# Attention layers 0 and 1: score stacks stored by half groups, loaded in rows of 8 KB

## The chip, the cores and the metric

The kernel runs on one core of one Trainium2 chip. The core has five engines with queues of their own: TensorE (PE, with its weight loads PEld), VectorE (DVE), ScalarE (ACT), GpSimd (POOL) and SyncE (SP), and 16 DMA engines. Transfers are issued by SP, ACT and POOL. The metric is the time of one execution on the device in microseconds (us), as the median of several.

## The reference

Four layers of gated cross-attention, each followed by a feed-forward part, over x of (32, 128, 128) in float32. What the change touches is the attention of layers 0 and 1 only: 16 heads of 8 elements, keys and values from the context, queries from the normalised x. Layer 0 turns queries and keys by their place (rotary), layer 1 does not.

```
q = proj(layernorm(x), Wq, bq)      # (32, 16, 128, 8)
k = proj(ctx, Wk, bk)
v = proj(ctx, Wv, bv)
attn = softmax(einsum('bhqd,bhkd->bhqk', q, k) / sqrt(8))
x = x + tanh(g) * (merge(attn @ v) @ Wo.T + bo)
```

## The kernel before

The 32 sequences are worked on in 8 groups (NG) of 4 (GS); a group has T = 512 columns, and HALF = 256 columns are two of its sequences. `heads_attention` is called once for layer 0 (`l0x`, with rope) and once for layer 1 (`l1x`). The five engines run programs written out by hand in this function, and meet by semaphores.

**Parts.** Scores are computed in bfloat16 at the precision of float32: keys and queries are each split into three bfloat16 parts (NPART = 3), and all nine products of a key part and a query part are summed in one matmul with a contraction over 3 x 3 x 8 = 72 rows (SROWS). So for each head a "stack" of 72 partitions is wanted, in which row (a, b, d) of the key stack holds part a of the keys and the same row of the query stack holds part b of the queries, for element d of the head. Three more rows (TROWS = 75) carry the negated maxima in the query stack, and ones in the key stack.

**How a stack is made.** The projection stands in `parts` as 128 partitions (d, head) x 3 parts x 512 columns. The reordering goes through DRAM. SP stores the parts into `scratch` and loads the stack from there. Keys are stored three times (L278), so that their three copies of a part lie where one load of 72 rows (L290) finds them; queries are stored once (L281), and a load of 24 rows is issued three times (L296). A load is made for each half group, and moves pieces of 256 columns of a head, 512 bytes. In SP's program for each group after the first stand: key store, key load of half 0, query store, query load of half 0, key load of half 1, query load of half 1. The load waits until the store of the whole group has landed (`s_stored`), and for the scores that read the same buffer two groups earlier (L288). In group 0 both key loads stand ahead of the query store, and after its loads of layer 0 SP issues the remaining 2.5 MB of x and context (L2740, L2745).

**Who uses it.** PE computes scores (L373: queries stationary, keys moving) three sequences ahead (LEAD), DVE takes the row maxima from them (L710), POOL splits the maxima into parts (L629 to L632), PE turns them (L399), ACT copies them out (L520) and issues a transfer of three rows into the query stack (L525). Then PE computes the transposed scores with the maxima already subtracted (L386), ACT takes the exponentials (L531), and PE multiplies by the values (L410). POOL splits the keys and queries of later groups (L615 to L621); in group 0 DVE does so (L698 to L703). `scores` waits at the first unit of each half group for `stack_landed` of keys and queries, and PE works strictly in order: everything behind a waiting L373 waits too.

Of the kernel before, what the change touches and what calls it, by code (L numbers as in the profile page):

```python
# [21 lines left out]
P = 128  # L22
# [143 lines left out]
def heads_attention(nc, k, name, rope, gain):  # L166
# [9 lines left out]
    with ExitStack() as ctx:  # L176
# [17 lines left out]
        parts = {n: sb(f"{n}_parts", [P, NPART, T], BF16) for n in "kq"}  # L194
        scratch = {"k": nc.dram_tensor(f"{name}_k_scratch", (2, NPART, NPART, P, T), BF16).ap(),
                   "q": nc.dram_tensor(f"{name}_q_scratch", (2, NPART, P, T), BF16).ap()}
        stack = {n: sb(f"{n}_stack", [TROWS, 2, HEADS, T], BF16) for n in "kq"}
        ones_row = sb("ones_row", [NPART, T], BF16)
# [31 lines left out]
        s_split = sem("split_step")  # L230
        s_stored = {n: sem(f"{n}_parts_in_dram") for n in "kq"}
        s_stack = {n: [[sem(f"{n}_stack_in_{p}_{hf}") for hf in range(2)] for p in range(2)] for n in "kq"}
# [20 lines left out]
        half = lambda hf: slice(hf * HALF, (hf + 1) * HALF)  # L253
        loads = {"k": 1, "q": NPART}
        stores = {"k": NPART, "q": 1}

# [3 lines left out]

        def parts_stored(eng, n, g):

            eng.wait_ge(s_stored[n], 16 * stores[n] * (g + 1))

# [3 lines left out]
        def _(sp):  # L268
            sp.wait_ge(s_fill, 4)
            sp.dma_start(stack["k"][SROWS:TROWS, :, :, :].rearrange("a p h t -> a (p h) t"),  # L270
                         bcast(ones_row[:, :].unsqueeze(1), [NPART, 2 * HEADS, T])).then_inc(s_ones, 16)

            def store(n, g):

                sp.wait_ge(s_parts[n], g + 1)
                if n == "k":
                    for b in range(NPART):
                        sp.dma_start(scratch["k"][g % 2, :, b].rearrange("a p t -> p a t"), parts["k"][:, :, :])\  # L278
                          .then_inc(s_stored["k"], 16)
                else:  # L280
                    sp.dma_start(scratch["q"][g % 2].rearrange("b p t -> p b t"), parts["q"][:, :, :])\  # L281
                      .then_inc(s_stored["q"], 16)

            def load(n, g, hf):

                parts_stored(sp, n, g)
                if g >= 2:
                    sp.wait_ge(s_T, 4 * (GS * (g - 2) + 2 * hf + 2))  # L288
                if n == "k":
                    sp.dma_start(stack["k"][0:SROWS, g % 2, :, half(hf)],  # L290
                                 scratch["k"][g % 2].rearrange("a b (d h) t -> (a b d) h t", h=HEADS)[:, :, half(hf)])\
                      .then_inc(s_stack["k"][g % 2][hf], 16)
                else:
                    rows_of_a = NPART * HD
                    for a in range(NPART):
# [23 lines left out]
        def _(pe):  # L319
# [43 lines left out]
            def scores(j, u):  # L363

                g, c = divmod(j, GS)
                if u == 0 and c % 2 == 0:
                    stack_landed(pe, "k", g, c // 2)
                    stack_landed(pe, "q", g, c // 2)
                if 4 * j + u >= 2:
                    pe.wait_ge(s_max, 4 * j + u - 1)  # L370
                for i in range(4):
                    h = 4 * u + i
                    ins = pe.matmul(bankS[u % 2][:, seq(i)], stack["q"][0:SROWS, g % 2, h, seq(c)],  # L373
                                    stack["k"][0:SROWS, g % 2, h, seq(c)], start=True, stop=True)
                ins.then_inc(s_S, 1)

            def scoresT(j, u):
# [6 lines left out]
                for i in range(4):  # L384
                    h = 4 * u + i
                    ins = pe.matmul(bankT[u % 2][:, seq(i)], stack["k"][:, g % 2, h, seq(c)],  # L386
                                    stack["q"][:, g % 2, h, seq(c)], start=True, stop=True)
                ins.then_inc(s_T, 1)
# [96 lines left out]
        def _(act):  # L485
# [36 lines left out]
            def max_rows(j):  # L522
                g, c = divmod(j, GS)
                act.wait_ge(s_mT, j + 1)
                act.dma_start(stack["q"][SROWS:TROWS, g % 2, :, seq(c)], mT[:, seq(c)]).then_inc(s_mrow[c], 16)  # L525

# [63 lines left out]
        def _(pool):  # L590
# [2368 lines left out]
```

## Time and profile before

| | |
|---|---|
| median of 3 runs | 1749.2 us (1742.07 to 1757.42) |
| the profiled execution | 1753.31 us, span 1751.5 us |
| granted TensorE clock over the span | 0.869 of full |
| busy: PE, DVE, ACT, POOL | 1434.0, 901.2, 510.1, 413.7 us |
| attention of layer 0 in the trace | from the start to about 265 us |
| attention of layer 1 | about 430 to 668 us |
| DMA | 134171 packets, 151.33 MB |

The remaining time belongs to the feed-forward parts and to layers 2 and 3. A wait of an engine is named by the line that waited and by what came last; "issue" there means that the profile found no releaser. The landing of the stack loads is not recorded for the loads of the later groups, only their issue on SP.

### The profile page before, as it was taken

How to read it: one execution, taken by the hardware profiler on the slowest of the kernel's cores; microseconds unless marked ns; L12 is line 12 of the kernel's file. 1: busy time of each engine (PE TensorE's matmuls, PEld its weight loads, DVE VectorE, ACT ScalarE, POOL GpSimd, SP SyncE). 2: the span in 40 equal slices, each digit the busy share in tenths (PEclk: the TensorE clock that was granted, in tenths of full speed). 3: DMA queues.
4: the chain of work that ended last, by engine and by line, in shares of the span. 5: the costliest groups of instructions: out<-in, count | busy, mean ns of one | idle time of the engine just before them, and what ended most of it. 6: DMA issues, size and time to landing. Idle time of an engine off the chain costs nothing. (4 is left out here: it accounts for less than half of the span.)

```text
span 1751.5 us, 26351 instructions
## 1 busy us (share of the span) xinstructions
PE 1434.0 (82%) x8869; PEld 909.0 (52%) x8869; DVE 901.2 (51%) x2554; ACT 510.1 (29%) x1195; POOL 413.7 (24%) x713
## 2 busy tenths in 40 slices
PE   4798886885688885897778669666699999999998
PEld 2577663443467673665677547444344443444443
DVE  4565646886356552433354433375544465455535
ACT  1455552111366652222443223243010110111001
POOL 2665710000466520000133322262000000000000
PEclk8698988997599877999575679888799999999999
DMA  6665650000667636700000011123222022022110
GB/s 179 170 160 136 147 132 1 1 0 7 170 154 165 155 87 241 312 0 8 23 19 20 21 46 56 46 66 109 97 97 103 1 102 103 25 78 103 60 43 12
DMA packets 134171, 151.33 MB, mean 86 GB/s; under 512 B 12150, under 2 KB 117942, under 8 KB 128806
## 3 DMA queue, kind: packets, MB, share of 16 engines
q1 hardware_dynamic: 127494, 142.28, 27.6%
q0 software_dynamic: 3296, 6.76, 1.3%
q8 instruction: 68, 1.11, 0.3%
q10 hardware_dynamic: 3264, 0.79, 0.2%
q14 instruction: 49, 0.40, 0.1%
HBM read 99.33 MB, written 49.48 MB: 85 GB/s over the span
## 5 line engine op out<-in xcount | busy, mean ns | idle before, releaser
L2596 DVE TENSOR_TENSOR l3f_weighted_T<-l3f_w_e,l3f_xnT 128x512 f32<-128x512 f32 x128 | 88.4, 691 | 129.8 <-PE psum L2347 115.0
L2347 PE MATMUL psum<-l3f_weighted_T,w_l3f_q 128*128 128x512 f32 x256 | 133.7, 604 | 16.2 <-DVE l3f_weighted_T L2596 14.4
L2347 PE MATMUL psum<-l3f_weighted_T,w_l3f_k 128*128 128x512 f32 x256 | 131.6, 596 | 0.0
L2347 PE MATMUL psum<-l3f_weighted_T,w_l3f_v 128*128 128x512 f32 x256 | 131.5, 595 | 0.0
L710 DVE TENSOR_REDUCE l1x_minus_max<-psum 128x4 f32<-128x512 f32 x128 | 85.9, 687 | 81.0 <-PE psum L373 79.7
L2356 PE MATMUL psum<-l3f_weighted_T,w_l3f_o 128*128 128x512 f32 x256 | 124.4, 624 | 1.7 <-DVE l3f_weighted_T L2596 1.7
L710 DVE TENSOR_REDUCE l0x_minus_max<-psum 128x4 f32<-128x512 f32 x128 | 85.4, 686 | 66.5 <-PE psum L373 65.9
L2596 DVE TENSOR_TENSOR l3f_weighted_T<-l3f_w_e,l3f_oT 128x512 f32<-128x512 f32 x128 | 88.4, 692 | 57.3 <-PE psum L2356 30.0
L531 ACT ACTIVATE l0x_probsT<-psum 128x512 f32<-128x512 f32 x128 | 73.6, 595 | 57.2 <-PE psum L386 49.8
L111 POOL TENSOR_TENSOR l3f_ln_rstd<-l3f_ln_mean_var,eps 128x4 f32<-128x4 f32 x8 | 1.9, 243 | 355.5 <-DVE l3f_ln_mean_var L104 355.5
L531 ACT ACTIVATE l1x_probsT<-psum 128x512 f32<-128x512 f32 x128 | 73.7, 593 | 36.4 <-PE psum L386 26.9
L2356 PEld LDWEIGHTS psum<-l3f_weighted_T,w_l3f_o 128*128 128x128 f32 x256 | 39.3, 188 | 82.9 <-DVE l3f_weighted_T L2596 78.2
L2347 PEld LDWEIGHTS psum<-l3f_weighted_T,w_l3f_k 128*128 128x128 f32 x256 | 48.9, 191 | 61.8 <-issue 61.8
L2347 PEld LDWEIGHTS psum<-l3f_weighted_T,w_l3f_v 128*128 128x128 f32 x256 | 48.9, 191 | 61.8 <-issue 61.8
L2347 PEld LDWEIGHTS psum<-l3f_weighted_T,w_l3f_q 128*128 128x128 f32 x256 | 44.6, 192 | 60.4 <-issue 44.4
L373 PE MATMUL psum<-l0x_k_stack,l0x_q_stack 72*128 72x128 bf16 x512 | 59.7, 250 | 15.9 <-DMA l0x_q_stack<-l0x_q_scratch 8.8
L373 PE MATMUL psum<-l1x_k_stack,l1x_q_stack 72*128 72x128 bf16 x512 | 57.7, 245 | 17.1 <-issue 10.4
L386 PE MATMUL psum<-l1x_q_stack,l1x_k_stack 75*128 75x128 bf16 x512 | 54.7, 237 | 2.3 <-DMA l1x_q_stack<-l1x_minus_max_T 2.3
L386 PE MATMUL psum<-l0x_q_stack,l0x_k_stack 75*128 75x128 bf16 x512 | 56.2, 241 | 0.5 <-DMA l0x_q_stack<-l0x_minus_max_T 0.5
L373 PEld LDWEIGHTS psum<-l0x_k_stack,l0x_q_stack 72*128 72x128 bf16 x512 | 41.5, 114 | 19.5 <-issue 16.2
L373 PEld LDWEIGHTS psum<-l1x_k_stack,l1x_q_stack 72*128 72x128 bf16 x512 | 40.1, 110 | 21.2 <-issue 18.4
L902 ACT ACTIVATE l0f_hT<-psum,w_l0f_cb 128x512 f32<-128x512 f32 x32 | 22.0, 687 | 99.3 <-PE psum L850 99.3
(480 smaller groups left out, 3034.5 us busy)
## 6 DMA issues: line engine op xcount, KB each, us to landing
l3f_w_e<-l3f_weights_scratch SPq DMA_DIRECT2D x32, 1024.0 KB, 4.6
sorted_x<-zeros SPq DMA_DIRECT2D x1, 16896.0 KB, 59.0
l0x_k_scratch<-l0x_k_parts SPq DMA_DIRECT2D x24, 384.0 KB, 3.8
l0x_k_stack<-l0x_k_scratch SPq DMA_DIRECT2D x16, 576.0 KB
l0x_q_stack<-l0x_q_scratch SPq DMA_DIRECT2D x48, 192.0 KB
l1x_k_scratch<-l1x_k_parts SPq DMA_DIRECT2D x24, 384.0 KB, 4.6
l1x_k_stack<-l1x_k_scratch SPq DMA_DIRECT2D x16, 576.0 KB
l1x_q_stack<-l1x_q_scratch SPq DMA_DIRECT2D x48, 192.0 KB
```

What stands on the lines that cost most here:

```text
L111: pool.tensor_tensor(k.rstd[:, :], k.mv[:, :, 1], k.eps[:, :], ALU.add).then_inc(k.s_vare, 1)
L373: ins = pe.matmul(bankS[u % 2][:, seq(i)], stack["q"][0:SROWS, g % 2, h, seq(c)], stack["k"][0:SROWS, g % 2, h, seq(c)], start=True, stop= ...
L386: ins = pe.matmul(bankT[u % 2][:, seq(i)], stack["k"][:, g % 2, h, seq(c)], stack["q"][:, g % 2, h, seq(c)], start=True, stop=True)
L531: act.activation(pT[:, j % 2, 4 * u:4 * u + 4, :], bankT[u % 2].rearrange("p (i q) -> p i q", i=4), ACT.Exp, scale=scale).then_inc(s_exp, 1)
L710: dve.tensor_reduce(nm[:, j % GS, 4 * u:4 * u + 4], bankS[u % 2].rearrange("p (i t) -> p i t", i=4), AX, ALU.max, negate=True).then_inc(s_ ...
L902: act.activation(hT[:, par, n, :], bankH[n % 2][:, :], ACT.Silu, bias=w["l0f_cb"][:, n:n + 1]).then_inc(r_act.sem, 1)
L2347: ins = pe.matmul(bank[:, :], w[name][:, e, :], xe[:, e % 2, :], start=(e == 0), stop=(e == NE3 - 1))
L2356: pe.matmul(bankO[g % 2][:, :], w["l3f_o"][:, e, :], xe[:, e % 2, :], start=(e == 0), stop=(e == NE3 - 1))\
L2596: dve.tensor_tensor(xe[:, e % 2, :], wE[:, g % 2, e, :], src, ALU.mult).then_inc(s_xe, 1)
```

## The change

Scratch and stacks get a dimension for the half group, so that all 16 heads of one half stand side by side: 16 x 256 columns of bfloat16 are one row of 8 KB, both in DRAM and in a partition of the stack. Stores go out by halves, each with a semaphore of its own. Keys are stored once. Queries are stored as five blocks, parts 0, 1, 2, 0, 1. A load of a half is three transfers of 24 rows for keys as for queries: for the keys three times parts 0, 1, 2; for the queries blocks s to s + 2, so parts (0, 1, 2), (1, 2, 0), (2, 0, 1). The nine pairs are complete, in another order. The matmuls read the same columns of a head from their new place.

```
-        scratch = {"k": nc.dram_tensor(f"{name}_k_scratch", (2, NPART, NPART, P, T), BF16).ap(),
-                   "q": nc.dram_tensor(f"{name}_q_scratch", (2, NPART, P, T), BF16).ap()}
-        stack = {n: sb(f"{n}_stack", [TROWS, 2, HEADS, T], BF16) for n in "kq"}
+        blocks = {"k": NPART, "q": 2 * NPART - 1}
+        scratch = {n: nc.dram_tensor(f"{name}_{n}_scratch", (2, 2, blocks[n], P, HALF), BF16).ap() for n in "kq"}
+        stack = {n: sb(f"{n}_stack", [TROWS, 2, 2, HEADS, HALF], BF16) for n in "kq"}
...
-                if n == "k":
-                    for b in range(NPART):
-                        sp.dma_start(scratch["k"][g % 2, :, b].rearrange("a p t -> p a t"), parts["k"][:, :, :])\
-                          .then_inc(s_stored["k"], 16)
-                else:
-                    sp.dma_start(scratch["q"][g % 2].rearrange("b p t -> p b t"), parts["q"][:, :, :])\
-                      .then_inc(s_stored["q"], 16)
+                for hf in range(2):
+                    to = scratch[n][g % 2, hf].rearrange("a p t -> p a t")
+                    sp.dma_start(to[:, 0:NPART, :], parts[n][:, :, half(hf)]).then_inc(s_stored[n][hf], 16)
+                    if n == "q":
+                        sp.dma_start(to[:, NPART:2 * NPART - 1, :], parts["q"][:, 0:NPART - 1, half(hf)])\
+                          .then_inc(s_stored["q"][hf], 16)
...
-                parts_stored(sp, n, g)
+                parts_stored(sp, n, g, hf)
...
-                if n == "k":
-                    sp.dma_start(stack["k"][0:SROWS, g % 2, :, half(hf)],
-                                 scratch["k"][g % 2].rearrange("a b (d h) t -> (a b d) h t", h=HEADS)[:, :, half(hf)])\
-                      .then_inc(s_stack["k"][g % 2][hf], 16)
-                else:
-                    rows_of_a = NPART * HD
-                    for a in range(NPART):
-                        sp.dma_start(stack["q"][a * rows_of_a:(a + 1) * rows_of_a, g % 2, :, half(hf)],
-                                     scratch["q"][g % 2].rearrange("b (d h) t -> (b d) h t", h=HEADS)[:, :, half(hf)])\
-                          .then_inc(s_stack["q"][g % 2][hf], 16)
+                rows_of = lambda ap: ap.rearrange("a (d h) t -> (a d) (h t)", h=HEADS)
+                block_rows = NPART * HD
+                for s in range(NPART):
+                    first = s if n == "q" else 0
+                    sp.dma_start(stack[n][s * block_rows:(s + 1) * block_rows, g % 2, hf, :, :]
+                                 .rearrange("r h t -> r (h t)"), rows_of(scratch[n][g % 2, hf, first:first + NPART]))                      .then_inc(s_stack[n][g % 2][hf], 16)
...
-                    ins = pe.matmul(bankS[u % 2][:, seq(i)], stack["q"][0:SROWS, g % 2, h, seq(c)],
-                                    stack["k"][0:SROWS, g % 2, h, seq(c)], start=True, stop=True)
+                    ins = pe.matmul(bankS[u % 2][:, seq(i)], stack["q"][0:SROWS, g % 2, c // 2, h, of_seq(c)],
+                                    stack["k"][0:SROWS, g % 2, c // 2, h, of_seq(c)], start=True, stop=True)
```

The transposed scores (L386) and ACT's transfer of the maxima (L525) are addressed in the same manner. POOL's wait for the stores of the group before (in `split`) becomes two waits, one for each half.

SP's queue at the start of layer 0, groups 0 and 1, before; `l0x_k_parts` are the split keys in SBUF, `l0x_k_scratch` their place in DRAM, and the numbers are partitions or rows x pieces x elements:

```order
L278 DMA l0x_k_scratch<-l0x_k_parts 128x3x512 x3
L290 DMA l0x_k_stack<-l0x_k_scratch 72x16x256 x2
L281 DMA l0x_q_scratch<-l0x_q_parts 128x3x512
L296 DMA l0x_q_stack<-l0x_q_scratch 24x16x256 x6
L2740 DMA x_sb<-in_x 128x2560
L2745 DMA ctxT<-in_ctxT 128x2560
L278 DMA l0x_k_scratch<-l0x_k_parts 128x3x512 x3
L290 DMA l0x_k_stack<-l0x_k_scratch 72x16x256
L281 DMA l0x_q_scratch<-l0x_q_parts 128x3x512
L296 DMA l0x_q_stack<-l0x_q_scratch 24x16x256 x3
```

The same place of the change:

```order
L279 DMA l0x_k_scratch<-l0x_k_parts 128x3x256 x2
L293 DMA l0x_k_stack<-l0x_k_scratch 24x4096 x6
L279 DMA l0x_q_scratch<-l0x_q_parts 128x3x256
L281 DMA l0x_q_scratch<-l0x_q_parts 128x2x256
L279 DMA l0x_q_scratch<-l0x_q_parts 128x3x256
L281 DMA l0x_q_scratch<-l0x_q_parts 128x2x256
L293 DMA l0x_q_stack<-l0x_q_scratch 24x4096 x6
L2737 DMA x_sb<-in_x 128x2560
L2742 DMA ctxT<-in_ctxT 128x2560
L279 DMA l0x_k_scratch<-l0x_k_parts 128x3x256 x2
L293 DMA l0x_k_stack<-l0x_k_scratch 24x4096 x3
```

The order of the kinds is unchanged. In each group SP issues 2 key stores instead of 3, 6 key loads instead of 2, 4 query stores instead of 1, and 6 query loads as before: 18 transfers instead of 12. The rows of PE, ACT, DVE and POOL stand in the same order before and after.

## Rows read from the trace of the kernel before

**Rows 1.** Waits, PE, 28 to 265 us: us in total, times, longest.
```profile
PE psum L373 <- DMA l0x_q_stack<-l0x_q_scratch: 8.8, 1, 8.8
...
PE psum L373 <- issue: 6.1, 2, 4.0
```

**Rows 2.** Waits, PE, 425 to 668 us.
```profile
PE psum L373 <- issue: 10.4, 3, 4.1
...
PE psum L373 <- DMA l1x_q_stack<-l1x_q_scratch: 5.6, 1, 5.6
...
PE psum L386 <- DMA l1x_q_stack<-l1x_minus_max_T: 2.3, 2, 1.4
```

**Rows 3.** Timeline, PE: start, us, instruction, count, idle before it and releaser.
```profile
38.39 1.01 PE L373 MATMUL psum<-l0x_k_stack,l0x_q_stack 72*128 72x128 bf16 x8 [8.82 <-DMA l0x_q_stack<-l0x_q_scratch]
...
65.25 0.58 PE L373 MATMUL psum<-l0x_k_stack,l0x_q_stack 72*128 72x128 bf16 x4 [3.95 <-issue]
...
458.08 1.01 PE L373 MATMUL psum<-l1x_k_stack,l1x_q_stack 72*128 72x128 bf16 x8 [5.64 <-DMA l1x_q_stack<-l1x_q_scratch]
...
504.14 0.43 PE L373 MATMUL psum<-l1x_k_stack,l1x_q_stack 72*128 72x128 bf16 x4 [4.00 <-issue]
```

**Rows 4.** Timeline, SP's queue at the start of layer 0.
```profile
16.64 1.63 SPq L278 DMA_DIRECT2D l0x_k_scratch<-l0x_k_parts  x3
21.53 1.70 SPq L290 DMA_DIRECT2D l0x_k_stack<-l0x_k_scratch  x2
23.86 2.53 SPq L281 DMA_DIRECT2D l0x_q_scratch<-l0x_q_parts  x1
31.63 4.78 SPq L296 DMA_DIRECT2D l0x_q_stack<-l0x_q_scratch  x6
36.45 0.54 SPq L2740 DMA_DIRECT2D x_sb<-in_x  x1
...
37.51 1.96 SPq L278 DMA_DIRECT2D l0x_k_scratch<-l0x_k_parts  x3
51.67 0.79 SPq L290 DMA_DIRECT2D l0x_k_stack<-l0x_k_scratch  x1
```

**Rows 5.** Timeline, SP's queue, one later group of layer 1.
```profile
484.08 2.60 SPq L278 DMA_DIRECT2D l1x_k_scratch<-l1x_k_parts  x3
489.54 0.78 SPq L290 DMA_DIRECT2D l1x_k_stack<-l1x_k_scratch  x1
490.69 0.47 SPq L281 DMA_DIRECT2D l1x_q_scratch<-l1x_q_parts  x1
496.88 2.40 SPq L296 DMA_DIRECT2D l1x_q_stack<-l1x_q_scratch  x3
```

**Rows 6.** Windows: busy us of each engine (instructions), granted clock, DMA share, GB/s.
```profile
24.00:28.00 4.00, 1.63 (x7) 0.72 (x6) 1.85 (x4) 0.70 (x2) 1.78 (x2) 1.00 0.92 217
34.00:38.00 4.00, 0.00 (x0) 0.00 (x0) 0.00 (x0) 0.00 (x0) 0.00 (x0) 0.50 0.88 168
39.00:49.00 10.00, 8.03 (x53) 5.61 (x51) 8.95 (x21) 0.87 (x2) 6.52 (x9) 0.50 1.04 364
231.00:241.00 10.00, 9.46 (x106) 7.14 (x105) 4.51 (x9) 3.93 (x9) 0.88 (x4) 0.51 1.08 216
581.00:589.00 8.00, 8.00 (x69) 5.59 (x68) 3.94 (x11) 2.90 (x7) 1.71 (x4) 0.50 0.99 232
590.00:620.00 30.00, 27.90 (x447) 23.12 (x444) 19.49 (x40) 22.96 (x51) 20.08 (x37) 1.00 0.63 153
```

**Rows 7.** The tile l0x_k_scratch: landing of its stores after their issue.
```profile
DMA to landing us min/median/max: 2.5/3.8/12.7
```

**Rows 8.** Timeline, POOL: the last step of a split of queries.
```profile
488.79 1.16 POOL L621 TENSOR_TENSOR l1x_q_parts<-l1x_rest,l1x_q_parts 128x512 bf16<-128x512 f32 x1
```

**Rows 9.** Line L525, transfers of maxima: durations of issue in ns, first and last start.
```profile
L525 ACTq DMA_DIRECT2D l0x_q_stack<-l0x_minus_max_T x32: 728/729/1368, 45.8 to 255.9; - x32
L525 ACTq DMA_DIRECT2D l1x_q_stack<-l1x_minus_max_T x32: 728/729/781, 465.5 to 656.0; - x32
```

More of the change, by code:

```diff
@@ L230, in heads_attention @@
         s_split = sem("split_step")
-        s_stored = {n: sem(f"{n}_parts_in_dram") for n in "kq"}
+        s_stored = {n: [sem(f"{n}_parts_in_dram_{hf}") for hf in range(2)] for n in "kq"}
         s_stack = {n: [[sem(f"{n}_stack_in_{p}_{hf}") for hf in range(2)] for p in range(2)] for n in "kq"}
@@ L253, in heads_attention, with parts_stored @@
         half = lambda hf: slice(hf * HALF, (hf + 1) * HALF)
-        loads = {"k": 1, "q": NPART}
-        stores = {"k": NPART, "q": 1}
+        of_seq = lambda c: slice((c % 2) * P, (c % 2 + 1) * P)
+        loads = {"k": NPART, "q": NPART}
+        stores = {"k": 1, "q": 2}
         def stack_landed(eng, n, g, hf):
             eng.wait_ge(s_stack[n][g % 2][hf], 16 * loads[n] * (g // 2 + 1))
-        def parts_stored(eng, n, g):
-            eng.wait_ge(s_stored[n], 16 * stores[n] * (g + 1))
+        def parts_stored(eng, n, g, hf):
+            eng.wait_ge(s_stored[n][hf], 16 * stores[n] * (g + 1))
         block = ctx.enter_context(nc.Block())
@@ L269, in _ @@
             sp.wait_ge(s_fill, 4)
-            sp.dma_start(stack["k"][SROWS:TROWS, :, :, :].rearrange("a p h t -> a (p h) t"),
-                         bcast(ones_row[:, :].unsqueeze(1), [NPART, 2 * HEADS, T])).then_inc(s_ones, 16)
+            sp.dma_start(stack["k"][SROWS:TROWS, :, :, :, :].rearrange("a p f h t -> a (p f h) t"),
+                         bcast(ones_row[:, 0:HALF].unsqueeze(1), [NPART, 4 * HEADS, HALF])).then_inc(s_ones, 16)
             def store(n, g):
                 sp.wait_ge(s_parts[n], g + 1)
-                if n == "k":
-                    for b in range(NPART):
-                        sp.dma_start(scratch["k"][g % 2, :, b].rearrange("a p t -> p a t"), parts["k"][:, :, :])\
-                          .then_inc(s_stored["k"], 16)
-                else:
-                    sp.dma_start(scratch["q"][g % 2].rearrange("b p t -> p b t"), parts["q"][:, :, :])\
-                      .then_inc(s_stored["q"], 16)
+                for hf in range(2):
[4 more added lines that the diff above has]
+                          .then_inc(s_stored["q"][hf], 16)
@@ L385, in scoresT @@
                     h = 4 * u + i
-                    ins = pe.matmul(bankT[u % 2][:, seq(i)], stack["k"][:, g % 2, h, seq(c)],
-                                    stack["q"][:, g % 2, h, seq(c)], start=True, stop=True)
+                    ins = pe.matmul(bankT[u % 2][:, seq(i)], stack["k"][:, g % 2, c // 2, h, of_seq(c)],
+                                    stack["q"][:, g % 2, c // 2, h, of_seq(c)], start=True, stop=True)
                 ins.then_inc(s_T, 1)
@@ L524, in max_rows @@
                 act.wait_ge(s_mT, j + 1)
-                act.dma_start(stack["q"][SROWS:TROWS, g % 2, :, seq(c)], mT[:, seq(c)]).then_inc(s_mrow[c], 16)
+                act.dma_start(stack["q"][SROWS:TROWS, g % 2, c // 2, :, of_seq(c)], mT[:, seq(c)]).then_inc(s_mrow[c], 16)
             def exps(j, u):
@@ L615, in split @@
                     step(pool.tensor_tensor(full[n][:, :], turned[n][0][:, :], turned[n][1][:, :], ALU.add))
-                parts_stored(pool, n, g - 1)
+                for hf in range(2):
+                    parts_stored(pool, n, g - 1, hf)
                 p = [parts[n][:, a, :] for a in range(NPART)]
@@ L638, in _ @@
             split("k", 1)
+            split("q", 1)
             split_max(0)
-            split("q", 1)
             split_max(1)
```

## The prediction

> **What bounds the kernel now.** I read first the waits of TensorE (PE) inside the two attention layers. In layer 0 (28 to 265 us) its largest single wait is 8.8 us for the first load of query rows, and "issue" stands for 6.1 us in two pieces [rows 1]. In layer 1 there are 5.6 us for the same first load and 10.4 us of "issue" in three pieces [rows 2]. "Issue" says that the profile found no releaser. The timeline of PE tells what those pieces are: each stands ahead of the L373 matmul that opens a half group, as at 65.25 and 504.14 us [rows 3] (the others at 230.17, 530.43 and 580.80), and L373 at that place waits for nothing but the landing of the key and query stacks and for a maximum that has long been taken. So these are loads too, whose landing the profile doesn't record. Together the loads cost PE 8.8 + 6.1 + 5.6 + 10.4 = 30.9 us. That is the reach of this change on the direct path; the other 1,250 us hold nothing that the diff touches.
>
> Second, SyncE (SP), which issues stores and loads in program order. At the start of layer 0 [rows 4]: the key load goes out at 21.53 us, the query store at 23.86, but the query load only at 31.63, 7.8 us after the store, because the store lies in the queues behind the two key loads; the first scores start 6.8 us later, at 38.39 [rows 3]. A steady group looks alike [rows 5]: key store 484.08, key load 489.54 (5.5 us), query store 490.69, query load 496.88 (6.2 us), use at 504.14 (7.3 us). From key store to scores that is 20.1 us.
>
> Third, the rates of the loads. With key loads of 72 rows in flight (24 to 28 us) the queues move 217 GB/s; with query loads of 24 rows alone (34 to 38) 168 GB/s at a busy share of 0.88; plain loads over 128 partitions in rows of 10 KB, beside a rest of the query loads (39 to 49), 364 GB/s [rows 6].
>
> **The change, part by part.**
> *Computation: 0.* The matmuls, their number and order stay; they read 128 adjacent columns before and after. The nine pairs of parts are taken in turned order, and this alters only the order of a sum.
>
> *Key store.* Three transfers of 384 KB become two of 192 KB. Today it takes 5.5 us until the load goes out [rows 5]; the quickest of the 24 landings was 2.5 us [rows 7]. With one issue ahead (about 0.5 us, the row of three took 1.6 to 2.6) I take 3.0 us. Gain 2.5 us for the key chain, bounds 1 and 3.
>
> *Query store.* 384 KB become 640 KB in four transfers, but the first half's load waits for 320 KB only. It still has the key load ahead of it in the queues. At the start, both halves of the key load do: 2 x 576 KB.
>
> *Loads.* Same bytes, 2 x 576 KB for each of keys and queries. Only the shape changes: 8 KB rows instead of 512 B pieces, but keys now in transfers of 24 rows too. The trace shows no 24-row transfer with long rows, so I bound it. Below: 168 GB/s, the row of 24-row loads, so 3.5 us for a half (keys today 2.7 us at 217). Above: 364 GB/s, 1.6 us. I take a value nearer the lower end, 220 GB/s, 2.7 us, since the nearest row in shape on the SBUF side is the query load. Issuing: six loads took 4.78 us [rows 4], 0.80 each; one flat 128-partition load took 0.54 [rows 4]. Keys now need three issues for a half instead of one: 3 x 0.54 - 0.80 = 0.8 us more, queries 0.8 us less. These cancel.
>
> The Trainium skill (SBUF — State Buffer, section on the DMA port swizzle) says that bandwidth follows the number of the 16 ports that the partitions reach, four neighbouring partitions to a port. Twenty-four rows then reach 6 ports and by its 27.2 GB/s for each at most 163 GB/s, whatever the row length; the 168 GB/s of the query loads agree. By that page this change makes the key loads slower, and the sum would be its low end below.
>
> *Start of layer 0 (wait 8.8).* Key load out at 16.64 + 3.0 = 19.6 instead of 21.5: 1.9 earlier [rows 4]. Its 1,152 KB (1.18 MB) take 5.4 us at 217 GB/s, 7.0 at 168: 1.6 lost at the low end; at 220 nothing changes. A query load of 0.59 MB at 168 takes 3.5 us; at 220, 2.7. And 0.3 us are saved since its first issue is shorter. Low: 1.9 - 1.6 + 0.3 = 0.6. At 220: 1.9 + 0.8 + 0.3 + about 0.5 for a store of 320 instead of 384 KB ahead of the load = 3.5. High, at 364: the query store is bound by its own time, 23.86 + 0.5 + 2.5 = 26.9, and from load to scores it takes 6.8 - 1.9 - 0.3 = 4.6: scores at 31.5, gain 6.9. Taken: **3.5**.
>
> *Second wait of layer 0 (3.95).* Group 1's key store goes out at 37.51 behind the 2.5 MB of x and context, and lands only for the load at 51.67 [rows 4]. This chain moves forward with the query loads, as PE does, and the key store has 768 KB less to carry: 0.79 MB at 364 GB/s, 2.2 us; the query load gives 1.1 more. Bounds 2 and 3.95, taken **3.3**.
>
> *Steady groups (2.1 in layer 0, 10.4 in layer 1).* From rows 5: key store 484.08, key load 487.1 instead of 489.54. Today the query store lands 496.88 - 489.54 = 7.3 us after the key load goes out, of which 1.4 are its start, 2.7 data and 3.2 tail; the query parts are ready at 488.79 + 1.16 = 489.95 [rows 8], before the key data end. Low end: 487.1 + 1.4 + 3.5 + 3.2 = 495.2, plus 7.3 - 0.3: use at 502.2 against 504.14, gain 2.0 for each. At 220: 487.1 + 7.3 = 494.4, plus 7.3 - 0.8 - 0.3: 500.6, gain 3.5. Each wait's own length (4.0, 2.3 and 4.1 in layer 1) caps it: layer 0 **2.1**; layer 1 3.5 + 2.3 + 3.5 = **9.3** (low 2.0 and 6.0, high 2.1 and 10.4).
>
> *Start of layer 1 (5.6).* Same chain as in layer 0, bounds 0.6 and 5.6, taken **3.2**.
>
> *Clock.* A load's wait is followed by a low stretch: 231 to 241 us with a granted clock of 0.51 and PE busy 9.46 of 10 us, 581 to 589 us at 0.50 and busy 8.00 of 8. From 590 to 620, where no load is waited for, it is 1.00 [rows 6]. At 1.2 instead of 2.4 GHz busy PE loses about half: 4.7 + 4.0 = 8.7 us in these two. Bounds: nothing (other engines hold PE, or the clock falls all the same), and 15 (the shorter low stretches as well). Taken: **8**.
>
> Sum: 3.5 + 3.3 + 2.1 + 3.2 + 9.3 + 8 = **29.4 us**. Against the profiled execution's own 1753.3 us (span 1751.5 and 1.8 around it) that is 1724; this execution lies 4.1 above the median 1749.2, so I forecast 1720 for the median. All low ends: 0.6 + 2 + 2.0 + 0.6 + 6.0 + 0 = 11, so 1738; all high ends: 6.9 + 4.0 + 2.1 + 5.6 + 10.4 + 15 = 44, so 1705.
>
> What covers the parts at nothing: four query stores instead of one (about 1.5 us more on SP) lie before the wait for their landing; the ones rows (192 pieces instead of 96) land long before L386 needs them. Without that cover the store would cost 1 us for each of 16 groups on the query chain, inside the slack won.
>
> **Rivals.**
> *The 24 rows bind all loads.* The row of 168 GB/s speaks for it, nothing but the row length against. Then the direct sum is 11, with most of the clock 17: 1732, at the edge of what can be told. Chance 0.16.
>
> *Another wait takes the place.* GpSimd splits the parts and maxima, and PE in layer 0 already waits for that. If PE's earlier arrival meets it, or the clock falls elsewhere, only the two starts and part of the second wait remain: 3.5 + 3.2 + 3, about 10: 1739. For it: GpSimd is busy 6.5 of 10 us from 39 to 49, right behind the first wait [rows 6]. Against: that leaves it a third of the stretch. Chance 0.16.
>
> *Slower: the rows of maxima come late.* Each sequence ACT issues a 12 KB transfer of 48 pieces of 256 B onto three partitions, so that one engine of the queues may have 16 of them. If each must let one 8 KB row pass instead of a 512 B piece, and such a row takes 8192 B / (364/16 GB/s) = 0.36 us, it takes 5.8 us longer. Today it already makes PE wait 2.3 us in two pieces of layer 1 [rows 2]; I estimate its landing at 4.8 us then. The transfers follow each other at (255.9 - 45.8)/31 = 6.8 us in layer 0 and (656.0 - 465.5)/31 = 6.1 in layer 1 [rows 9], and its use is about 1.4 sequences behind its issue: 9.5 and 8.6 us. A landing of 10.6 is late by 1.1 and 2.0. If half of the sequences meet loads, 16 x 3.1 = 50 us are lost, 29 won: 1770. It decides from a landing of about 9 us on. Against it: rows don't reach further than the backlog of loads, which empties no later than today. Chance 0.10. The Trainium skill (DMA: Bandwidth & Descriptors, section on queues, rings and completion order) says that an engine takes turns between its queue rows packet by packet, a packet being several descriptors; that is this rival's mechanism, and no row here shows it with 8 KB rows.
>
> *Loads at the full rate and a clock that stays up.* 44 us or more: 1705. Chance 0.08.
>
> **How the numbers follow.** The forecast has 0.50, the others as given. About 1% (17 us) is what a measurement of this kernel can tell from no change. Faster by over 1%: 0.50 + 0.08 and half of the first rival, 0.08: 0.66. Within 1%: its other half and the second rival: 0.24. Slower: 0.10. The range of 8 in 10 runs from 1702, just beyond the high ends, to 1743, beyond the second rival, and leaves out the slower one.
>
> **What would show it.** Right: SP's query load goes out under 7 us after the query store at the first group of layer 0; key store to key load about 3 us; the idle ahead of L373 at the openings of half groups shrinks from 30.9 us to under 10; clock 1.00 where 0.5 stood at 231 and 581 us. Wrong: load stretches below 160 GB/s, or L386 idle for the rows of maxima over 10 us, or the same low stretches with no wait ahead of them. The forecast fails mostly if GpSimd or the clock gives the won time back.

## The result and the profile after

The changed kernel takes 1724.9 us, median of 4 runs (1722.0 to 1730.4), against 1753.3 us (1742.1 to 1759.7, 4 runs) before: a ratio of 0.9855, 95% interval 0.9813 to 0.9897. Run again on another chip it gave 1719.0 us and 0.9824 (0.9768 to 0.9879). Of both I call the change 1.5 to 1.8% faster: 25 to 31 us, where 29.4 were forecast.

The waits of TensorE after the change, layer 0 (28 to 255 us) and layer 1 (405 to 645 us); the columns are as in [rows 1, 2]. L369 and L382 are L373 and L386 of before.

```profile
PE psum L382 <- DMA l0x_q_stack<-l0x_minus_max_T: 3.2, 3, 2.4
...
PE psum L369 <- issue: 3.0, 1, 3.0
...
PE psum L369 <- DMA l0x_q_stack<-l0x_q_scratch: 1.9, 1, 1.9
...
PE psum L382 <- DMA l1x_q_stack<-l1x_minus_max_T: 7.9, 5, 2.9
...
PE psum L369 <- DMA l1x_q_stack<-l1x_q_scratch: 1.8, 1, 1.8
```

The waits for loads fell from 30.9 to 1.9 + 3.0 + 1.8 and 0.4 of "issue" in layer 1 = 7.1 us. The waits for rows of maxima rose from 2.8 (2.3 of [rows 2] and 0.5 in layer 0) to 3.2 + 7.9 = 11.1 us. So 15.5 us of waiting were won on balance, not 24. The second execution has 9.4 us for loads and 11.6 for maxima, 12.7 us less than before.

Two profiles of the same kernel, and that of before, by stage: layer 0 from 28 us to its end, layer 1 from its start to its end. The columns are those of [rows 6]. First before:

```profile
28.00:277.00 249.00, 198.31 (x2438) 153.69 (x2436) 138.13 (x319) 119.26 (x261) 126.42 (x231) 0.83 0.60 144
436.00:680.00 244.00, 192.84 (x2432) 149.07 (x2432) 125.09 (x307) 132.84 (x288) 113.03 (x224) 0.81 0.59 140
```

then the changed kernel,

```profile
28.00:271.00 243.00, 201.71 (x2442) 154.84 (x2442) 137.85 (x317) 120.14 (x262) 128.41 (x232) 0.83 0.53 132
430.00:655.00 225.00, 182.28 (x2432) 142.47 (x2432) 124.02 (x306) 132.53 (x288) 113.23 (x224) 0.86 0.55 133
```

and its second execution, on the other chip:

```profile
28.00:264.00 236.00, 193.40 (x2438) 149.53 (x2438) 137.55 (x317) 119.76 (x262) 127.47 (x232) 0.86 0.53 136
423.00:646.00 223.00, 178.71 (x2432) 139.51 (x2432) 124.50 (x307) 133.13 (x288) 113.63 (x225) 0.87 0.55 134
```

Layer 1 has the same 2,432 matmuls in all three. It is 19 and 21 us shorter: PE's busy time fell by 10.6 and 14.1 us (a granted clock of 0.86 and 0.87 against 0.81), its idle time by 8.4 and 6.9. Layer 0 ends at 271.1 and 264.4 us instead of 276.6, so 5.5 us earlier in one profile and 12.2 in the other; its busy time rose by 3.4 in the one and fell by 4.9 in the other. What layer 0 won is thus uncertain by some 7 us from one profile alone. Of the kernel before there is one profile only, and its executions lie between 1738.7 and 1763.3 us, so its 0.81 is uncertain too. All behind the end of layer 1 takes as long as before (1071.7, 1072.3 and 1072.2 us). Packets fell from 134,171 to 74,716, bytes from 151.3 to 143.0 MB.

SP's queue at the start of layer 0, to be read against [rows 4]:

```profile
16.91 0.93 SPq L279 DMA_DIRECT2D l0x_k_scratch<-l0x_k_parts  x2
19.04 2.36 SPq L293 DMA_DIRECT2D l0x_k_stack<-l0x_k_scratch  x6
22.93 0.39 SPq L279 DMA_DIRECT2D l0x_q_scratch<-l0x_q_parts  x1
...
28.96 2.34 SPq L293 DMA_DIRECT2D l0x_q_stack<-l0x_q_scratch  x6
...
33.92 0.94 SPq L279 DMA_DIRECT2D l0x_k_scratch<-l0x_k_parts  x2
45.05 1.13 SPq L293 DMA_DIRECT2D l0x_k_stack<-l0x_k_scratch  x3
```

The key load follows its store by 2.1 us (4.9 before), the query load by 6.0 (7.8). Six loads are issued in 2.3 us where they took 4.8. The last two rows are the second group: its key load still waits 11.1 us, since its store lies behind the 2.5 MB of x and context (14.2 before). A later group of layer 1, against [rows 5]:

```profile
473.57 0.91 SPq L279 DMA_DIRECT2D l1x_k_scratch<-l1x_k_parts  x2
...
477.10 1.16 SPq L293 DMA_DIRECT2D l1x_k_stack<-l1x_k_scratch  x3
...
479.47 0.38 SPq L279 DMA_DIRECT2D l1x_q_scratch<-l1x_q_parts  x1
...
483.63 1.89 SPq L293 DMA_DIRECT2D l1x_q_stack<-l1x_q_scratch  x3
```

3.5 us from key store to key load (5.5 before) and 4.2 from query store to query load (6.2 before). What PE does at the places of [rows 3]:

```profile
34.70 0.61 PE L369 MATMUL psum<-l0x_k_stack,l0x_q_stack 72*128 72x128 bf16 x8 [1.87 <-DMA l0x_q_stack<-l0x_q_scratch]
...
57.68 0.59 PE L369 MATMUL psum<-l0x_k_stack,l0x_q_stack 72*128 72x128 bf16 x4 [2.99 <-issue]
...
227.73 0.61 PE L382 MATMUL psum<-l0x_q_stack,l0x_k_stack 75*128 75x128 bf16 x4 [2.43 <-DMA l0x_q_stack<-l0x_minus_max_T]
...
612.92 0.40 PE L382 MATMUL psum<-l1x_q_stack,l1x_k_stack 75*128 75x128 bf16 x4 [2.88 <-DMA l1x_q_stack<-l1x_minus_max_T]
```

First scores stand at 34.70 instead of 38.39, 3.7 us earlier, though the wait ahead of them shrank by 6.9 (8.8 to 1.9). The other 3.3 us are no gain: PE came to this wait later, because it did the projection ahead of it at a granted clock of 0.50, where before it had 1.00. The rows before and after:

```profile
27.62 1.96 PE L325 MATMUL psum<-l0x_xnT,w_l0x_projections 128*128 128x512 f32 x4 [0.78 <-ACT l0x_xnT L509]
```
```profile
29.40 3.44 PE L321 MATMUL psum<-l0x_xnT,w_l0x_projections 128*128 128x512 f32 x4 [0.78 <-ACT l0x_xnT L505]
```

In the second execution this clock was 1.00, the wait 4.4 us and the first scores at 35.04.

The last of the rows at PE's places (612.92) is the new wait at its longest. The queues of ACT and of SP tell how it comes about:

```profile
602.84 0.76 ACTq L521 DMA_DIRECT2D l1x_q_stack<-l1x_minus_max_T  x1
```
```profile
599.38 1.13 SPq L293 DMA_DIRECT2D l1x_q_stack<-l1x_q_scratch  x3
600.61 1.12 SPq L293 DMA_DIRECT2D l1x_k_stack<-l1x_k_scratch  x3
601.83 1.12 SPq L293 DMA_DIRECT2D l1x_q_stack<-l1x_q_scratch  x3
```

The maxima's 12 KB go out at 602.84, with nine loads of 192 KB issued in the 3.5 us before, and are used at 612.92: 10.1 us, of which PE, ready at 610.04, had 7.2 to spare. From 603 to 609 us SP's queue (q1) moved data and ACT's (q10), which carries the maxima, none; from 609 to 613 it moved two of their transfers. The first row is q1 in the first stretch, the second q10 in the second:

```profile
q1 hardware_dynamic: 176, 0.96, 77.8%
```
```profile
q10 hardware_dynamic: 102, 0.02, 3.5%
```

By the packets of the trace the first of the 48 pieces moved at 609.5, 6.6 us after the issue, and the last landed at 612.0, 9.1 us after it. The Trainium skill (DMA: Bandwidth & Descriptors, section on queues, rings and completion order) says that an engine takes turns between its queue rows packet by packet. The trace doesn't show that here: for 6.6 us the loads went ahead without a piece of the maxima between them. What held the pieces back isn't shown. Late landings are few: the median of the 64 transfers is 2.1 us in layer 0 and 2.6 in layer 1, where it was 3.7 and 3.1 before; the longest is 9.1, where it was 8.0.

Windows at loads and at the low stretches:

```profile
30.00:33.00 3.00, 2.84 (x4) 0.68 (x2) 0.12 (x1) 0.00 (x0) 2.77 (x4) 0.50 0.69 172
55.00:61.00 6.00, 3.32 (x45) 2.39 (x45) 2.29 (x4) 0.91 (x2) 4.37 (x4) 0.67 0.76 156
228.00:238.00 10.00, 9.46 (x96) 7.62 (x97) 4.45 (x9) 4.50 (x9) 0.88 (x4) 0.50 0.55 153
561.00:571.00 10.00, 10.00 (x153) 7.90 (x151) 8.11 (x24) 7.70 (x17) 7.50 (x14) 1.00 0.40 86
```

Query loads alone in flight (30 to 33 us) move 172 GB/s, a later stretch of loads 156. The granted clock still falls to 0.50 at 228 us, now behind a wait for maxima; in the second execution it is low there only from 225.5 to 228.9. At 561 us stands the half group that had 0.50 at 581 before: it has 1.00 now. One more long low stretch of before went away:

```profile
620.00:641.00 21.00, 19.56 (x196) 15.55 (x196) 9.89 (x20) 7.98 (x17) 2.63 (x12) 0.51 0.53 110
```

No load was waited for ahead of it: from 608 to 641 us PE's waits were 0.5 us three times and 0.7 once. In the changed kernel the clock is low only from 613.4 to 616.8 between 552 and 647 us.

### The profile page after: what moved, and what is told of

The parts are those of the page before. It is cut to its first block and busy times, and to the rows that moved or that the text cites. A ratio compares the mean times of both kernels' runs of the same rounds, so it can differ in the third digit from the quotient of the medians.

```text
span 1727.5 us, 26460 instructions
## 1 busy us (share of the span) xinstructions
PE 1429.1 (83%) x8869; PEld 906.0 (52%) x8869; DVE 900.6 (52%) x2554; ACT 510.2 (30%) x1195; POOL 415.3 (24%) x713
## 2 busy tenths in 40 slices
DMA packets 74716, 142.96 MB, mean 83 GB/s; under 512 B 13430, under 2 KB 53878, under 8 KB 64742
## 5 line engine op out<-in xcount | busy, mean ns | idle before, releaser
L527 ACT ACTIVATE l1x_probsT<-psum 128x512 f32<-128x512 f32 x128 | 73.3, 593 | 27.9 <-PE psum L382 18.3
L369 PE MATMUL psum<-l0x_k_stack,l0x_q_stack 72*128 72x128 bf16 x512 | 58.8, 248 | 6.3 <-issue 3.0
L382 PE MATMUL psum<-l0x_q_stack,l0x_k_stack 75*128 75x128 bf16 x512 | 55.8, 240 | 3.2 <-DMA l0x_q_stack<-l0x_minus_max_T 3.2
L382 PE MATMUL psum<-l1x_q_stack,l1x_k_stack 75*128 75x128 bf16 x512 | 51.7, 228 | 7.9 <-DMA l1x_q_stack<-l1x_minus_max_T 7.9
L369 PE MATMUL psum<-l1x_k_stack,l1x_q_stack 72*128 72x128 bf16 x512 | 54.7, 236 | 3.2 <-DMA l1x_q_stack<-l1x_q_scratch 1.8
L1893 DVE TENSOR_TENSOR l_h_tile<-psum,w_l2f_b 128x512 f32<-128x512 f32 x39 | 27.0, 692 | 41.1 <-PE psum L1529 40.0
L369 PEld LDWEIGHTS psum<-l0x_k_stack,l0x_q_stack 72*128 72x128 bf16 x512 | 40.9, 112 | 10.1 <-issue 6.5
```

The lines of the kernel that those rows point to most:

```text
L527: act.activation(pT[:, j % 2, 4 * u:4 * u + 4, :], bankT[u % 2].rearrange("p (i q) -> p i q", i=4), ACT.Exp, scale=scale).then_inc(s_exp, 1)
L1893: dve.tensor_tensor(hp[:, u % 2, :], bankU[u % 2][:, :], w["l2f_b1"][:, bass.ds(e * HID, HID)], ALU.add)\
```

## The experiments

The change has four parts: keys stored once, stores and loads by halves, keys loaded as three transfers of 24 rows, and rows of 8 KB. The third is only tried together with the first. Every kernel below computes all that the kernel before does. Each ratio is to the kernel before timed on the same chip (medians 1749.5 to 1753.3 us). In one table, with PE's waits in the stretches of the two layers (for loads, and for rows of maxima, in us) and the length of layer 1:

| kernel | keys once | halves | rows | us | ratio to before (95%) | loads | maxima | layer 1 |
|---|---|---|---|---|---|---|---|---|
| before | no | no | 512 B | | 1 | 30.9 | 2.8 | 244.2 |
| e2_keys_once | yes | no | 512 B | 1738.1 | 0.9934 (0.9898-0.9969) | 23.6 | 0.2 | 234.3 |
| e9_halves_only | no | yes | 512 B | 1732.4 | 0.9895 (0.9850-0.9941) | 24.2 | 6.7 | 232.6 |
| e3_long_rows | no | yes | 8 KB | 1730.9 | 0.9884 (0.9813-0.9956) | 9.7 | 16.1 | 230.3 |
| e1_short_rows | yes | yes | 512 B | 1721.1 | 0.9832 (0.9760-0.9903) | 18.3 | 2.5 | 228.3 |
| after | yes | yes | 8 KB | 1724.9 | 0.9855 (0.9813-0.9897) | 7.1 | 11.1 | 225.6 |
| after_again | yes | yes | 8 KB | 1719.0 | 0.9824 (0.9768-0.9879) | 9.4 | 11.6 | 222.8 |
| e10_rows_4k | yes | yes | 4 KB | 1708.1 | 0.9752 (0.9700-0.9804) | 10.6 | 1.9 | 215.0 |

**Short rows.** All of the change but the long rows: the scratch in DRAM keeps a stride of 512 columns, so each piece is 512 B again.

```diff
-        scratch = {n: nc.dram_tensor(f"{name}_{n}_scratch", (2, 2, blocks[n], P, HALF), BF16).ap() for n in "kq"}
+        scratch = {n: nc.dram_tensor(f"{name}_{n}_scratch", (2, 2, blocks[n], P, T), BF16).ap() for n in "kq"}
...
-                rows_of = lambda ap: ap.rearrange("a (d h) t -> (a d) (h t)", h=HEADS)
+                rows_of = lambda ap: ap.rearrange("a (d h) t -> (a d) h t", h=HEADS)
```

> The changed kernel with one thing put back: the scratch rows in DRAM get a stride, so that each load again moves pieces of 512 B (24 x 16 x 256) instead of rows of 8 KB; keys stored once, halves, turned pairs and the layout of the stack stay. Theory A (the short key store gives the gain; the rate of a 24-row load is bound at about 165 GB/s whatever its pieces): between 1720 and 1730 us, first scores of layer 0 within 1.5 us of 34.7, and PE's waits for the rows of maxima (L382) fall from 11.1 us (3.2 in layer 0, 7.9 in layer 1) to under 5. Theory B (the long rows give the gain): 1740 us or more, first scores at 37 us or later. SP's issues grow from 0.39 to 0.8 us a load in both.

1721.1 us, ratio 0.9832: the gain is all there without the long rows. Its waits, layer 0 and then layer 1:

```profile
PE psum L370 <- DMA l0x_q_stack<-l0x_q_scratch: 4.4, 1, 4.4
PE psum L370 <- issue: 3.2, 1, 3.2
PE psum L383 <- DMA l0x_q_stack<-l0x_minus_max_T: 0.8, 1, 0.8
...
PE psum L370 <- issue: 7.6, 3, 3.8
PE psum L370 <- DMA l1x_q_stack<-l1x_q_scratch: 3.1, 1, 3.1
PE psum L383 <- DMA l1x_q_stack<-l1x_minus_max_T: 1.7, 1, 1.7
```

Loads cost 18.3 us of waits and maxima 2.5, where 8 KB rows have 7.1 and 11.1. The long rows do shorten the loads' waits, by 11.2 us, and give 8.6 of them back at the maxima. The 2.6 us between them are less than these measurements tell apart. SP issues six such loads in 4.8 us, not 2.3.

**Keys stored once, nothing else.** Before, with the keys stored once and loaded three times, the queries' scratch in five blocks; whole groups, old layout.

```diff
-        loads = {"k": 1, "q": NPART}
-        stores = {"k": NPART, "q": 1}
+        loads = {"k": NPART, "q": NPART}
+        stores = {"k": 1, "q": 2}
...
-                if n == "k":
-                    for b in range(NPART):
-                        sp.dma_start(scratch["k"][g % 2, :, b].rearrange("a p t -> p a t"), parts["k"][:, :, :])\
...
+                sp.dma_start(to[:, 0:NPART, :], parts[n][:, :, :]).then_inc(s_stored[n], 16)
```

> The kernel before with one part of the change alone: keys stored once, queries as five blocks, three loads of 24 rows for keys too; stores of whole groups, pieces of 512 B, and the old layout of the stack. Theory A: most of the gain, 1725 to 1735 us; key store to key load about 3.5 us instead of 5.5. Theory B: no gain, 1745 us or more, since keys are loaded in three transfers at the old rate.

1738.1 us, median of 10 runs, a few us slower than expected; ratio 0.9934. The key load goes out 2.5 us after the first key store and the first scores stand at 36.83 us. This part alone is worth 0.7%. In its profile layer 1 is 9.9 us shorter than before, yet waits for loads there fell only from 16.0 to 15.5 us and those for maxima by 2.3: most of it is busy time, 183.6 instead of 192.8 us.

**Long rows and halves, keys stored three times.** The changed kernel with six key stores of 192 KB, and one key load of 72 rows of 8 KB.

```diff
-        loads = {"k": NPART, "q": NPART}
-        stores = {"k": 1, "q": 2}
+        loads = {"k": 1, "q": NPART}
+        stores = {"k": NPART, "q": 1}
```

> The other part alone: halves and rows of 8 KB, but keys stored three times (six stores of 192 KB in a group) and loaded in one transfer of 72 rows, queries stored once. Theory A: 1740 to 1752 us, key store to key load still 5 us or more, waits for the rows of maxima as large as in the changed kernel. Theory B: most of the gain, 1725 to 1735 us. If the port of four neighbouring partitions is the bound and not the row, the 72-row load runs at over 200 GB/s and the 24-row ones at 165.

1730.9 us, below the 1740 to 1752 that the theory of keys stored once gave it: so something beside the keys brings 1%. Its waits for maxima are the longest of all:

```profile
PE psum L381 <- DMA l0x_q_stack<-l0x_minus_max_T: 5.1, 2, 2.6
...
PE psum L381 <- DMA l1x_q_stack<-l1x_minus_max_T: 11.0, 6, 2.7
```

Its key load is the only one with 72 long rows. In two stretches only packets of 8 KB, so these loads alone, are in flight, and both are faster than the 172 GB/s of 24 long rows:

```profile
23.00:24.00 1.00, 1.00 (x2) 0.48 (x3) 0.64 (x3) 1.00 (x4) 0.00 (x0) 0.50 0.75 205
27.00:28.00 1.00, 0.00 (x0) 0.00 (x0) 0.92 (x2) 0.00 (x0) 0.00 (x1) 1.00 0.76 188
```

**Halves alone.** The same with pieces of 512 B, so that only the split by halves is left against before.

```diff
-        scratch = {n: nc.dram_tensor(f"{name}_{n}_scratch", (2, 2, blocks[n], P, HALF), BF16).ap() for n in "kq"}
+        scratch = {n: nc.dram_tensor(f"{name}_{n}_scratch", (2, 2, blocks[n], P, T), BF16).ap() for n in "kq"}
```

> The third part alone: stores and waits by half groups, keys still stored three times (six stores of 192 KB), one key load of 72 rows, pieces of 512 B, queries stored once. The runs so far: keys once alone 0.993 of before, halves with long rows 0.988, halves with keys once 0.983, all three 0.986. Theory C (the wait for half of the stores is the main part): 0.988 to 0.992, 1729 to 1735 us; key store to key load 3.5 us as with the long rows. Theory D (the long rows did the work in the run with keys stored three times, by faster loads): 0.995 to 1.0, 1740 us or more, with waits for loads in layer 1 near the 10.4 us of before.

1732.4 us, median of 10; ratio 0.9895. With the halves alone the load waits for 3 of 6 stores, and key store to key load takes 3.5 us. Halves (0.9895) times keys once (0.9934) is 0.9830, and short rows, which have both, measured 0.9832: the two parts add up, and between 512 B and 8 KB nothing is left. PE's waits explain this kernel only in part: they sum to 30.9 us against 33.7, yet its profiled span is 14 us shorter (1737.3 against 1751.5). The window of its layer 1 shows where:

```profile
432.00:665.00 233.00, 184.15 (x2432) 142.87 (x2432) 125.03 (x308) 133.15 (x288) 113.34 (x225) 0.84 0.65 147
```

Busy time is 8.7 us less than before for the same matmuls, at a clock of 0.84 against 0.81, and idle time 2.3 less. Why the clock is higher with nearly as much waiting isn't settled.

**The weights of other layers later.** In layer 0 SP waits for the last rows of maxima before it issues the weights of the layers behind (L2796).

```diff
+            sp.wait_ge(s_mrow[GS - 1], 16 * NG)
```

> The changed kernel, with SP waiting for the last sequence's row of maxima before it issues the other layers' weights (35 transfers), in both attention layers. Theory: at the end of layer 0 the row of maxima waits behind these weights (2.43 us at 227.73, followed by a low clock), and that is where half of layer 0's gain went; then layer 0 ends 3 to 6 us earlier, 1719 to 1722 us in all. Rival: the lost time at the end is the clock alone, which falls anyway: then 1724 to 1726; if the first weights of layer 0's feed-forward part come too late, 1728 or more.

1717.8 us, 0.9826 (0.9751 to 0.9901). The 2.43 us at 227.73 are gone (layer 0's waits for maxima: 3.2 to 0.6), so these weights were their cause. Layer 0 ends at 267.4 us, between the 271.1 and 264.4 of the changed kernel's two profiles, so the 3 to 6 us expected there are not shown. In the total it can't be told from the changed kernel's 0.9824.

**Order at the start.** The first half's query store and load stand ahead of the second half's key load.

```diff
-            load("k", 0, 1)
...
+            load("k", 0, 1)
```

> The changed kernel with group 0 in the order of the other groups on SP: the query store and first query load ahead of the second key load. In it the query store lies behind half of the key bytes only. Theory (the store waits in the queues behind the key loads): query store to query load falls from 6.0 to under 4 us, first scores at 33 us or earlier instead of 34.7, where PE has finished the projection; 1 to 2 us in all. Rival (it is the landing itself): 6 us stay.

One run, 1722.2 us. The query load follows its store by 2.6 us instead of 6.0 (23.22 to 25.78), so it was the second key load that held it. The first scores stand at 31.97 instead of 34.70 and wait for nothing, but the second group then waits longer:

```profile
31.97 0.80 PE L369 MATMUL psum<-l0x_k_stack,l0x_q_stack 72*128 72x128 bf16 x8
...
57.81 0.58 PE L369 MATMUL psum<-l0x_k_stack,l0x_q_stack 72*128 72x128 bf16 x4 [3.86 <-issue]
```

It stands at 57.81, no earlier than the 57.68 of the changed kernel: the 2.7 us were given back there. Layer 0 ends at 271.2.

**x and context later.** Their 2.5 MB are issued behind the loads of the second group.

```diff
-            if name == "l0x":
-                k.load_x(sp, 3)
-                k.load_ctx(sp, 3)
...
+                if name == "l0x" and g == 1:
+                    k.load_x(sp, 3)
+                    k.load_ctx(sp, 3)
```

> The changed kernel with the rest of x and context (2.5 MB) issued after group 1's first key and query loads instead of ahead of its key store. Theory (these 2.5 MB hold the second wait): key store to key load of group 1 falls from 11.1 to under 4 us, the wait of 2.99 us at 57.68 is gone, layer 0 ends 2 to 4 us earlier. Rival: GpSimd's split is late by then and another wait of 2 us or more takes the place, the end of layer 0 stays within 1 us.

One run, 1721.0 us. The second group's key load follows its store by 2.9 us instead of 11.1, and the load's wait is gone. The 2.5 MB now meet the next transfer of maxima, and layer 0 ends at 269.7 us, 1.4 before the changed kernel's first profile. So the rival was right that another wait takes the place, though it is one for maxima and not for GpSimd:

```profile
59.37 0.61 PE L382 MATMUL psum<-l0x_q_stack,l0x_k_stack 75*128 75x128 bf16 x4 [3.95 <-DMA l0x_q_stack<-l0x_minus_max_T]
```

**Rows of 4 KB.** If 8 KB rows help the loads but hold up the maxima, a size between the two should have both. Each load becomes two transfers, of eight heads each.

```diff
-        loads = {"k": NPART, "q": NPART}
+        loads = {"k": 2 * NPART, "q": 2 * NPART}
...
+                    for part in (slice(0, HEADS // 2 * HALF), slice(HEADS // 2 * HALF, HEADS * HALF)):
```

> The changed kernel with each load in two transfers of 8 heads: rows of 4 KB, twice the issues. If the rows of maxima take turns with the load's rows, their waits (L382: 3.2 and 7.9 us) fall to under 7 in all, while loads stay at the same rate; 0.36 us more for each issue delay the first scores by about 1 us. Sum: 1720 to 1726 us. If the waits stay at 11 us, it is not the size of the rows but the number of bytes ahead of them.

1708.1 us, ratio 0.9752 (0.9700 to 0.9804). Its waits:

```profile
PE psum L372 <- DMA l0x_q_stack<-l0x_q_scratch: 4.6, 1, 4.6
PE psum L372 <- issue: 3.7, 1, 3.7
PE psum L385 <- DMA l0x_q_stack<-l0x_minus_max_T: 1.0, 1, 1.0
...
PE psum L372 <- DMA l1x_q_stack<-l1x_q_scratch: 1.9, 1, 1.9
PE psum L385 <- DMA l1x_q_stack<-l1x_minus_max_T: 0.9, 1, 0.9
```

Maxima cost 1.9 us instead of 11.1, loads 10.6, nearly all of it at the two starts and the second group. Its four runs (1701 to 1710 us) lie below all runs of the kernels with 512 B and with 8 KB. Its layer 1 takes 215.0 us, with 177.4 of PE busy.

With these rows the loads also come as twice as many transfers, and that is a rival for what the length of the rows is credited with. SP issues nine loads of 192 KB in 3.6 us with 8 KB rows (599.38 to 602.95), while moving them at 172 GB/s takes 10 us; with 4 KB rows the issues take 8.5 us (562.04 to 570.51), with 512 B pieces 8.2 (574.56 to 582.79). So fewer bytes may stand ahead of the maxima because they are issued slower, whatever their rows. The two kernels with one key load of 72 rows, which go out fastest, speak for it: maxima cost 16.1 us there and not 11.1 with 8 KB, 6.7 and not 2.5 with 512 B (though they also store three times as many key bytes). Row length and pace of issue weren't tried apart.

**The changed kernel once more**, on the chip of the next one.

> The changed kernel once more, so that it and the next one are timed on one chip: 0.98 to 0.99 of before. Its waits for the rows of maxima are 11 us again within 3, and it still has the wait for loads of about 3 us in group 1 of layer 0; if they change by more than that, the differences between single profiles of the earlier runs say less than was read from them.

1719.0 us, 0.9824. The same waits within 1 us but for the first load's, 4.4 instead of 1.9 us, to which PE came 2.2 us earlier at its full clock.

**4 KB rows with the three moves together** (order at the start, x and context later, weights later).

> All that helped together: rows of 4 KB, group 0 in the order of the other groups, the rest of x and context after group 1's first loads, the other layers' weights after the last row of maxima. From the single runs: first scores 1 to 2 us earlier than the 33.2 of the 4 KB run, the wait of 3.7 us in group 1 gone, 2 us at the end of layer 0: 3 to 7 us below 1708, so 1701 to 1705 us, 0.971 to 0.973 of before. If the parts hide one another (GpSimd's splits as the next bound at the start), within 2 us of 1708.

1705.2 us, ratio 0.9756 (0.9713 to 0.9799), median of 6: no gain over the 4 KB rows alone that can be told. The first scores stand at 30.98 and no load is waited for over 2.3 us. But a row of maxima is late right behind, as with x and context moved alone:

```profile
60.57 0.40 PE L386 MATMUL psum<-l0x_q_stack,l0x_k_stack 75*128 75x128 bf16 x4 [3.11 <-DMA l0x_q_stack<-l0x_minus_max_T]
```

Its six runs and the four with 4 KB rows alone (1701 to 1713 us) lie below all eight of the changed kernel (1714 to 1730).

## Why the prediction was right, and where it wasn't

The size came out: 28 us by the medians of the first comparison, 29.4 forecast. Its steps one by one, with the second execution behind the stroke:

- **Start of layer 0, 3.5:** right, first scores 3.7 / 3.4 us earlier. Key store to key load took 2.1 us, where 3.0 stood; the query load still waited 6.0 us behind both key loads, as the prediction has it.
- **Second wait of layer 0, 3.3:** wrong. It shrank from 3.95 to 2.99 / 2.56, by 1.0 to 1.4. The prediction took 2.2 us for a lighter key store and 1.1 for the query load ahead of it, and the store's side of it came true: its load followed after 11.1 us instead of 14.2, still behind the 2.5 MB, and went out 6.6 us earlier in all. What failed is where PE stands then: it reached the wait at 54.69 instead of 61.30, also 6.6 us earlier, 3.7 by the start and 2.9 by less waiting and a higher clock in between (0.57 against 0.52). Moving these bytes took the wait away, and put one of 3.95 for maxima in its place.
- **Steady wait of layer 0, 2.1:** gone as a load's wait, but 2.43 stand at 227.73 for a row of maxima, behind the weights of the next layers. No step had asked what else is in the queues then.
- **Start of layer 1, 3.2:** right, 5.64 to 1.81 / 2.1.
- **Steady waits of layer 1, 9.3:** 10.0 of the 10.4 went, but perhaps not by the loads alone. The same loads in 512 B pieces left 7.6 us; in 8 KB rows the waits for maxima that came instead (7.9 against 2.3) may also hide what is left of them, which no run shows. On balance these won 10.4 + 2.3 - 0.4 - 7.9 = 4.4 us, about half of the term.
- **Clock, 8:** 7.2 / 19.0 us of busy time, so right in size in one profile and above its high bound of 15 in the other, and half wrong in place. Of the two stretches that it was worked out from, the one at 581 us came to 1.00, as named; the one at 231 stayed at 0.50 (for 3.4 us only in the second). Layer 1 gave it: 10.6 / 14.1 us less busy time. Layer 0 gave -3.4 / 4.9. And "a load's wait is followed by a low stretch" is not the whole cause: the 21 us from 620 followed none, and two kernels with nearly the old waits gained 9 us of busy time in layer 1.

In sum the direct waits won 15.5 / 12.7 us (12.2 in the first without the 3.3 by which PE only came later), not 21.4, and busy time 7.2 / 19.0 instead of 8. The forecast total was right partly since these two misses cancel, and that is luck. The signs: both times in SP's queue and the waits for loads (7.1 / 9.4 us, under 10) came as named. Against it stood PE's waits for maxima over 10 us, and one stretch of loads at 156 GB/s.

**Rates.** Query loads alone ran at 172 GB/s, other windows with loads from 156 up, nearer the low end (168) than the 220 taken. The first rival's premise held then: 8 KB rows don't speed a load of 24 rows. Its result (1732) didn't. But its 11 us of direct waits are at least as near to the 15.5 / 12.7 measured as the forecast's 21.4; what it lacked is busy time. The Trainium skill (SBUF — State Buffer, DMA port swizzle) gives 163 GB/s for the 6 ports of 24 rows; the windows of 24-row loads lie 5 to 9% above it (172 and 178 below); 72 rows alone moved 205 and 188.

**The slower rival was real and 6 times too dear.** Its landing of 10.6 us was measured once as 10.1 until use and 9.1 until the last piece landed, but not by its mechanism, turns taken between pieces and rows: for 6.6 us no piece moved at all. PE idles for maxima over 10 us, the sign that it named. What failed is "if half of the sequences meet loads, 16 x 3.1 = 50 us": the waits are 8 in number, 11.1 us in all, 8.3 more than before. I gave each sequence 8.6 to 9.5 us until its use (7.2 in the case measured) and counted 16 as late; most transfers don't meet nine loads issued at once, and half of them land within 2.6 us. The late ones make PE wait up to 2.4 us in layer 0 and 2.9 in layer 1, where 1.1 and 2.0 were forecast.

**Issuing.** "These cancel" was too careful: a flat load of 24 rows is issued in 0.36 to 0.39 us, not 0.54, so at the start the query loads save 2.4 us of SP's time (4.78 to 2.34) and the key loads cost 0.7 more (1.70 to 2.36).

## What to carry to other kernels

Look at the smallest urgent transfer that shares the queues with a bulk transfer before sizing the latter's rows or issuing it in one go: 8 KB rows won 11 us at the loads and gave back 9 at 48 pieces of 256 B, and 4 KB rows in twice as many transfers kept two thirds of the first without the second. A load that waits only for the part of a store that it reads was worth at least as much here (1.0%) as a store with a third of the bytes (0.7%). When a wait for a load goes, look for the next one behind it: two moves that each took one away were followed by another of 3.9 us. And don't take the size of a wait for the size of a gain: it also shrinks when the engine comes to it later.

## What the runs showed of the hardware

Loads of 24 rows move about the same whatever their pieces. A window with 4 KB rows and one with 512 B pieces, each with query loads alone in flight; 8 KB rows moved 172 too (30 to 33 us above):

```profile
30.00:33.00 3.00, 0.00 (x0) 0.00 (x0) 0.02 (x1) 0.00 (x0) 2.84 (x3) 0.77 0.77 172
```
```profile
33.00:35.00 2.00, 0.00 (x0) 0.00 (x0) 0.00 (x0) 0.00 (x0) 1.92 (x2) 0.97 0.89 178
```

I had expected more of a piece 8 to 16 times as long. The number of rows counted for a little: 188 and 205 GB/s with 72 of 8 KB.

Two executions of one kernel ended layer 0 at 271.1 and 264.4 us. A difference of 6 us between two single profiles is thus no evidence here. One cause shows at the start: the projection took 3.44 us in one and 1.96 in the other, at granted clocks of 0.50 and 1.00.

The granted clock of layer 1 is higher in each kernel of the table (0.84 to 0.87) than in the one profile of before (0.81), also where PE waits almost as long as before. Shorter waits are not the whole of it, and what else stays open.
